# Own attention of layers 0 and 2 in slots of several batches, and the beginnings of the tiled attention stages

## The chip, the cores and the metric

One core of one Trainium2 chip runs the whole kernel. A core has five engines that run their own instruction lists and meet only at semaphores: TensorE (PE in the profile; its weight loads stand apart as PEld), VectorE (DVE), ScalarE (ACT), GpSimd (POOL) and SyncE (SP), which issues the DMAs. TensorE writes eight banks of PSUM (0 to 7), from which VectorE and ScalarE read. The metric is the time of one execution on the device, in microseconds.

## What is computed

A decoder of four layers on `x` of 8 batches, 112 positions and 256 features, all in float32, with a context `ctx` of 8 × 375 × 128. Each layer adds own attention, cross attention and a feed-forward part, each on a layer norm of `x`. The parts that the change touches:

```python
# layer 0, own attention: 16 query heads, 4 key/value heads of 64
v = hn @ Wv.T + bv
q = relu(lstm_q(hn) @ Wq1.T + bq1) @ Wq2.T + bq2
k = relu(lstm_k(hn) @ Wk1.T + bk1) @ Wk2.T + bk2
k, v = repeat(k, 4), repeat(v, 4)
scores = where(causal, q @ k.T / 8, lowest)
y = concat(softmax(scores) @ v) @ Wo.T

# layer 2, own attention: 8 query heads, 4 key/value heads of 128, no bias
q, k, v = hn @ Wq, hn @ Wk, hn @ Wv
q, k = q * cos + rotate_half(q) * sin, k * cos + rotate_half(k) * sin
scores = where(causal, q @ repeat(k, 2).T / sqrt(128), -inf)
y = concat(softmax(scores) @ repeat(v, 2)) @ Wo
```

Of the other stages (own attention of layer 1, cross attention of layers 1 and 3, the two attention blocks of layer 2) the change touches the order of their first batch alone.

## The kernel before

**Stages.** The program is one stage after another. In a stage, a class gives one list of steps (`order()`), each a name with a batch and an index, and every engine walks through the same list and issues its own part of each step: `pe()`, `act()`, `dve()` and `pool()` of `Attention`. So the list sets the order on every engine, and semaphores hold an engine until the other one's part is done. `k.project` (L248) is a sum of matmuls over the feature tiles, `k.tp` (L253) a transpose on TensorE. One matmul in float32 stands as two instructions in the profile, one transpose as one. `k.next_bank` gives out the banks of a ring and waits until the last reader of that bank is done; `k.fill` does so for a fixed bank.

**Own attention of layers 0 and 2** (`L0Attn`, `L2Attn`, both on `Attention`). A batch's heads are taken in groups of four (4 groups in layer 0, 2 in layer 2). For a group: *scores* on TensorE into bank 0 or 1, 448 wide; *weigh*: VectorE adds the triangle to the four heads and writes them to memory (L639), takes the negated maxima (L645), and ScalarE computes four exponentials of 112x112 with their sums (L592); *turn*: four transposes of the weights (L253) into bank 4 or 5 and VectorE's copy (L659); *values*: the turned weights are TensorE's stationary side, the values move, and the result has queries on its partitions (banks 6 and 7). After a batch's last group, *divide* takes the reciprocals of the sums (L676) and scales the result out of the banks (L698, one instruction per bank of 512); *oT* turns it by eight transposes, copied by VectorE (L705); *y* multiplies with the output weights (two matmuls of 8 tiles, 256 moving, L248), and VectorE adds it to `x` (L756). The parts of the next batch (the *prologue*) and the end of the last one (the *epilogue*) are dealt by `Slots` over the gaps between these steps. The next batch's first group of scores stands ahead of the last group's values:

```python
            if b + 1 < B:
                yield from self.scoring(b + 1, 0, None)
            yield "values", b, self.G - 1
            yield "divide", b, 0
```

*Layer 0's prologue:* hid twice (112 positions by 64 on TensorE, relu on VectorE, L1480), queries twice (four tiles of 128 with a contraction of 64, L1456), keys (L1463) and v (L248). The contraction of the scores is 64 deep, while a tile of the queries holds two heads on 128 partitions. So VectorE writes each query tile twice, once with the one head and once with the other zeroed (L1486, scalar `q_mask`), and the score product takes all 128 rows. Keys are L1493. The scale of 1/8 is in the mask.

*Layer 2's prologue:* stats (VectorE, L764 to L769, then GpSimd's power, L790), xn (L774), xT (two transposes, copy L777), three rotations of four heads each (products of 128 x 112 on TensorE; VectorE two half-height products with sine, L1735, and one with cosine, L1737; GpSimd the sum, L1744), and v (512 wide). Scores of batch b wait for all three sums of b.

**Tiled stages** (`Tiled`: cross attention of layers 1 and 3, `L2Block2`; `TiledSelf`: `L1Attn`, `L2Block1`). Their heads of 16 or 32 are taken four at a time by row pieces of 32 for scores (L886, L1134) and column pieces of 32 for values (L912, L1158), with exponentials from L934 and L1174. The list has a *prologue* for batch 0, the first scores, then *second*, which is always of batch 1, then the loop with a *plan* of what goes into each gap. In `prologue`, k with an index is a piece of the keys, v a chunk of the values, vv two chunks at once. `dve_parity` (L1020 to L1028) begins stages with heads of 16: VectorE makes a mask for even and odd heads, then zeroes both value buffers (L1025, 128x1536 elements each in a cross stage, 112x512 in layer 1's attention), ahead of the first statistics. Queries are evacuated twice, once per parity (L1040). L1007 is GpSimd's copy that shares out the reciprocals, L1218 its product of 112x448, and L1182 ScalarE's copy of turned weights.

## Time and profile before

| | |
|---|---|
| median of 3 runs | 2730.49 us (2727.94 to 2737.71) |
| profiled execution | 2720.24 us, span 2718.4 us |
| mean granted clock | 0.828 of full |
| TensorE busy (PE / weight loads) | 2137.2 us (79%) / 1549.3 us |
| VectorE | 1506.7 us (55%) |
| ScalarE | 816.4 us (30%) |
| GpSimd | 336.0 us (12%) |
| chain that ended last | PE 60%, issue 16%, DVE 15%, POOL 3%, ACT 3%, DMA 2% |

The busy shares are means over stages that are bound differently, so they tell little of one stage. The chain (followed back from the last instruction to what released each step) is TensorE for six tenths and VectorE for three twentieths. The granted clock is TensorE's: 1 is full, 2.4 GHz, and 0.5 its lower level, 1.2 GHz; the mean of 0.828 holds stretches at either. Times in the trace count from the start of the span.

### The profile page before, as it was taken

Reading aid. Unit: us, or ns where it says so; the run is one execution under the profiler, and the core shown is the slowest. Engines: PE = TensorE matmul, PEld = TensorE weight load, DVE = VectorE, ACT = ScalarE, POOL = GpSimd, SP = SyncE. Lnnn points to the kernel's source line nnn. Section 1 sums busy time; section 2 is a strip of 40 time slices with the busy share of each in tenths; the row PEclk is TensorE's granted clock in tenths of the full one; section 3 lists DMA queues with packets and bytes.
Section 4 is the critical chain, followed back from the end, with each engine's and each line's share of the span. In section 5 each row is a group of like instructions: output and inputs, shape, how many; then the busy total and the mean of one; then the engine's idle time right before and its main releaser. Section 6 shows DMA issues by size and latency. Waiting matters only on the chain.

```text
span 2718.4 us, 56558 instructions
## 1 busy us (share of the span) xinstructions
PE 2137.2 (79%) x22836; PEld 1549.3 (57%) x22836; DVE 1506.7 (55%) x4047; ACT 816.4 (30%) x2897; POOL 336.0 (12%) x601
## 2 busy tenths in 40 slices
PE   7788888896777789478777387799889999879824
PEld 4777777774446566345666265566554544546612
DVE  5777776653424578643465264277617040358788
ACT  1333333221214556211111044156411111226511
POOL 2111111000000100000111153033100000210011
PEclk9555555987988889689899698899999999769956
DMA  2000001003000000200000200000011000000000
GB/s 116 4 4 4 4 4 67 1 1 141 14 0 1 7 10 10 117 0 1 4 1 1 124 1 1 6 10 8 4 72 59 0 0 0 1 9 13 5 0 14
DMA packets 7744, 57.14 MB, mean 21 GB/s; under 512 B 760, under 2 KB 5216, under 8 KB 5728
## 3 DMA queue, kind: packets, MB, share of 16 engines
q1 hardware_dynamic: 7488, 53.54, 5.1%
q8 instruction: 184, 3.01, 0.5%
q14 instruction: 72, 0.59, 0.1%
HBM read 52.62 MB, written 0.92 MB: 20 GB/s over the span
## 4 chain that ended last, share of the span: by engine, by line
PE 60%; issue 16%; DVE 15%; POOL 3%; ACT 3%; DMA 2%; POOLq 0%; DVEq 0%; SPq 0%; ACTq 0%
PE banks L248 35%; PE banks L1292 11%; PE banks L253 8%; PE banks L886 2%; PE banks L912 2%; DVE memory L1191 1%; ACT memory L934 1%; DVE memory L774 1%; DVE memory L972 1%; DMA memory<-in_l2x_rows 1%; DVE memory L698 1%; DVE memory L2302 1%; DVE memory L1394 1%; DVE memory L764 1%; PE banks L1456 1%
## 5 line engine op out<-in xcount | busy, mean ns | idle before, releaser
L248 PE MATMUL banks<-memory 128*128 128x448 f32 (+10 forms) x5040 | 1288.1, 412 | 123.6 <-DMA memory<-in_ctxT 16.9
L248 PEld LDWEIGHTS banks<-memory 128*128 128x128 f32 (+4 forms) x5040 | 828.8, 199 | 492.6 <-issue 260.1
L253 PE MATMUL banks<-memory 112*125 112x112 f32 (+3 forms) x2128 | 346.3, 296 | 249.9 <-DVE memory L774 124.2
L253 PEld LDWEIGHTS banks<-memory 112*125 112x125 f32 (+3 forms) x2128 | 264.2, 177 | 372.0 <-issue 185.1
L1292 PE MATMUL banks<-memory 128*128 128x8 bf16 (+2 forms) x10752 | 306.2, 174 | 75.8 <-DVE memory L1394 74.4
L1292 PEld LDWEIGHTS banks<-memory 128*128 128x128 bf16 x10752 | 295.3, 104 | 87.4 <-DVE memory L1394 85.3
L934 ACT ACTIVATE memory<-banks,memory 112x375 f32<-112x375 f32 x384 | 215.1, 578 | 17.2 <-DVE memory L972 17.1
L972 DVE TENSOR_REDUCE memory<-banks 112x2 f32<-112x750 f32 x192 | 171.1, 934 | 50.0 <-PE banks L886 48.1
L592 ACT ACTIVATE memory<-memory 112x112 f32<-112x112 f32 x192 | 72.1, 376 | 262.4 <-DVE memory L645 262.4
L790 POOL TENSOR_TENSOR memory<-memory 112x1 f32<-112x1 f32 x88 | 48.3, 549 | 790.0 <-DVE memory L769 788.5
L980 DVE COPY memory<-banks 125x448 f32<-125x448 f32 x192 | 116.7, 619 | 14.5 <-PE banks L253 10.2
L1377 DVE TENSOR_REDUCE memory<-banks 128x64 f32<-128x256 f32 x224 | 95.1, 425 | 27.5 <-PE banks L1292 1.6
L1316 ACT ACTIVATE memory<-memory 128x64 f32<-128x64 f32 x224 | 57.4, 256 | 171.7 <-DVE memory L1377 171.7
L886 PE MATMUL banks<-memory 32*112 32x375 f32 x768 | 89.8, 537 | 16.4 <-ACT memory L934 15.9
L1341 POOL TENSOR_SCALAR memory<-memory 128x16 f32<-128x16 f32 x224 | 59.8, 267 | 344.0 <-DVE memory L1394 344.0
L956 ACT COPY memory<-banks 125x448 f32<-125x448 f32 x96 | 51.1, 532 | 136.5 <-PE banks L253 136.5
L2659 DVE TENSOR_TENSOR memory<-banks,memory 112x256 f32<-112x256 f32 x8 | 3.4, 425 | 159.5 <-PE banks L248 159.5
L1174 ACT ACTIVATE memory<-banks,memory 112x112 f32<-112x112 f32 x256 | 86.2, 390 | 4.8 <-DVE memory L1191 3.4
L934 ACT ACTIVATION_READ_ACCUMULATOR memory<-banks,memory 112x1 f32 x384 | 80.6, 210 | 0.0
L912 PE MATMUL banks<-memory 125*32 125x112 f32 x2304 | 76.8, 267 | 1.4 <-DVE memory L980 1.4
L606 ACT COPY memory<-banks 128x375 f32<-128x375 f32 (+1 forms) x56 | 27.2, 485 | 150.7 <-PE banks L248 150.7
L2637 ACT ACTIVATE memory<-banks,memory 128x448 f32<-128x448 f32 x32 | 20.3, 633 | 173.5 <-PE banks L248 173.5
(202 smaller groups left out, 2126.4 us busy)
## 6 DMA issues: line engine op xcount, KB each, us to landing
memory<-in_l2x SPq DMA_DIRECT2D x1, 7680.0 KB, 21.2
memory<-in_l2f SPq DMA_DIRECT2D x1, 7168.0 KB, 19.6
memory<-in_l1f SPq DMA_DIRECT2D x1, 4617.0 KB, 17.0
memory<-in_ctxT SPq DMA_DIRECT2D x24, 187.5 KB
memory<-in_l0a SPq DMA_DIRECT2D x1, 4224.0 KB, 15.8
memory<-in_l2f SPq DMA_DIRECT2D x1, 4096.0 KB, 12.9
memory<-in_l3f SPq DMA_DIRECT2D x1, 3073.0 KB, 22.1
memory<-in_l2a SPq DMA_DIRECT2D x1, 3072.0 KB, 23.9
```

The source lines that it names most:

```text
L248: ins = self.nc.tensor.matmul(out, weights[i], acts[i], start=i == 0, stop=i == n - 1)
L253: return self.nc.tensor.transpose(out, in_, self.ident[0:n, 0:n])
L592: A.activation(P_sb[:, h, :], src[:, h, :], ACT.Exp, bias=u["nmax"][:, n + h:n + h + 1], scale=1.0, accum_out=u["total"][:, n + h:n + h + ...
L886: ins = PE.matmul(k.bank(bank, S, CK), q, kT, start=True, stop=True)
L912: ins = PE.matmul(k.banks[32 * r:32 * r + 32, 6, t * S:(t + 1) * S], v, PT_sb[0:CR, c, r * S:(r + 1) * S], start=c == 0 and m == 0, stop=c ...
L934: self.nc.scalar.activation(self.P_both[gi % 2][:, r, :], self.k.bank(r, S, CK), ACT.Exp, bias=u["nmax"][:, 4 * i + r:4 * i + r + 1], scal ...
L972: V.tensor_reduce(u["nmax"][:, 4 * i + 2 * h:4 * i + 2 * h + 2], k.banks[0:S, 2 * h:2 * h + 2, 0:CK], AX, ALU.max, negate=True).then_inc(* ...
L980: V.tensor_copy(self.PT_both[gi % 2][0:CR, c, :], k.bank(k.at["turn", gi, c], CR, 4 * S)).then_inc(*s.pt_v.up())
L1174: A.activation(self.P_all[:, i, g, :], k.bank(i, S, 4 * S)[:, g * S:(g + 1) * S], ACT.Exp, bias=u["nmax"][:, 4 * i + g:4 * i + g + 1], sca ...
L1292: ins = self.nc.tensor.matmul(self.slots[l][:, part:3, g * B:(g + 1) * B], whh[:, part, l, j, g * P:(g + 1) * P], self.upper[l][:, 0:3 - p ...
L1341: G.tensor_scalar(self.hs[:, l, :, :, t], self.h[:, l, 0].rearrange("p (k b) -> p k b", k=KD), 0.5, None, ALU.mult).then_inc(*s.h_kept.up())
L1377: V.tensor_reduce(self.sums[:, l], self.slots[l].rearrange("p s c -> p c s"), AX, ALU.add).then_inc(*s.gates_in.up())
```

## The change

**A new class `Causal`** carries both attentions. Its unit is eight heads: half a batch in layer 0, a whole one in layer 2. The steps of several batches stand in one slot (a tuple of step, index, and lag in batches), and the slot is repeated.

```diff
+class Causal(Attention):
...
+        self.ring = (2, 3, 4, 5)
...
+            if step == "sc":
...
+                for h in range(2):
+                    k.fill(h, s.exp_done(8 * n + 4 * h + 4))
+                    PE.matmul(k.bank(h, S, 4 * S), k.ident[0:S, 0:S],
+                              k.causal[0:S, :].unsqueeze(1).broadcast_to([S, 4, S]), start=True, stop=False,
+                              skip_group_check=True)
+                for j in range(4):
+                    for h in range(2):
+                        q, kT = self.score(b, i, h, j)
+                        ins = PE.matmul(k.bank(h, S, 4 * S)[:, j * S:(j + 1) * S], q, kT, start=False, stop=True,
+                                        skip_group_check=True)
+                ins.then_inc(*s.sc_full.up())
+            elif step == "turn":
+                for h in range(2):
+                    PE.wait_ge(*s.diag_ready(2 * n + h + 1))
+                    bank = k.next_bank(("turn", n, h), s.pt_ready(2 * n + h + 1))
+                    for j in range(4):
+                        ins = PE.matmul(k.bank(bank, S, 4 * S)[:, j * S:(j + 1) * S], self.P[n % 2][:, h, j, :],
+                                        self.diag[n % 2][:, h, j, :], start=True, stop=True)
+                    ins.then_inc(*s.pt_full.up())
...
+            if step == "exp":
+                for h in range(2):
+                    A.wait_ge(*s.nmax_ready(2 * n + h + 1))
+                    if n >= 2:
+                        A.wait_ge(*s.pt_full(2 * (n - 2) + h + 1))
+                        A.wait_ge(*s.inv_ready(n - 1))
+                    for j in range(4):
+                        at = 4 * h + j
+                        A.activation(self.P[n % 2][:, h, j, :], k.bank(h, S, 4 * S)[:, j * S:(j + 1) * S], ACT.Exp,
+                                     bias=self.nmax[n % 2][:, at:at + 1], scale=1.0,
+                                     accum_out=self.total[n % 2][:, at:at + 1]).then_inc(*s.exp_done.up())
...
+            if step == "max":
+                V.wait_ge(*s.sc_full(n + 1))
+                for h in range(2):
+                    V.tensor_reduce(self.nmax[n % 2][:, 4 * h:4 * h + 4],
+                                    k.bank(h, S, 4 * S).rearrange("p (h n) -> p h n", h=4), AX, ALU.max,
+                                    negate=True).then_inc(*s.nmax_ready.up())
+            elif step == "inv":
+                V.wait_ge(*s.exp_done(8 * (n + 1)))
+                if n >= 2:
+                    V.wait_ge(*s.diag_ready(2 * (n - 1)))
+                V.reciprocal(self.inv[n % 2], self.total[n % 2]).then_inc(*s.inv_ready.up())
...
+            if step == "inv":
+                G.wait_ge(*s.inv_ready(n + 1))
+                for h in range(2):
+                    if n >= 2:
+                        G.wait_ge(*s.pt_full(2 * (n - 2) + h + 1))
+                    G.tensor_tensor(self.diag[n % 2][:, h], k.ident[0:S, 0:S].unsqueeze(1).broadcast_to([S, 4, S]),
+                                    self.inv[n % 2][:, 4 * h:4 * h + 4].unsqueeze(2).broadcast_to([S, 4, S]),
+                                    ALU.mult).then_inc(*s.diag_ready.up())
```

So the triangle is written to the bank by a product with the identity, 448 wide, and the score products add to it; exponentials read the bank; the weights are multiplied by a diagonal matrix of the reciprocals, which turns and divides them at once; and the diagonals are made by GpSimd, a product of 112x448 with both operands broadcast. P, diag, nmax, total and inv have two buffers each, PT has one. The ring is banks 2 to 5.

**Layer 0.** The slot of a batch has an even and an odd unit. Scores and values use half the array: the two heads of a tile are row pieces of 64 in the scores, and column pieces of 64 in the values, so that the result has features on its partitions and needs no turning. VectorE writes the queries once.

```diff
+class L0Attn(Causal):
...
+    EVEN = (("y", 0, 3), ("turn", 0, 2), ("sc", 0, 1), ("max", 0, 1), ("exp", 0, 1), ("hid", 0, 0), ("hid", 1, 0),
+            ("values", 0, 2), ("queries", 0, 0), ("inv", 0, 1))
+    ODD = (("turn", 1, 2), ("sc", 1, 1), ("max", 1, 1), ("exp", 1, 1), ("keys", 0, 0), ("values", 1, 2),
+           ("queries", 1, 0), ("v", 0, 0), ("inv", 1, 1))
...
         self.w, self.bias, self.hs = lstm.w, lstm.bias, lstm.hs
...
-        self.o, self.oT = take(4 * D, parts=S), take(8, S)
-        self.q_mask, self.bq2m = take(2), take(2, 8)
-        self.take_common(take, [dict(qm=take(8, 2, S), kT=take(4, S), v=take(1, D, parts=S)) for _ in range(2)])
...
+        self.r1, self.bq2s = take(2, S, parts=64), take(8)
+        self.q, self.kT = [take(8, S) for _ in range(2)], [take(4, S) for _ in range(2)]
+        self.v, self.oT = [take(D, parts=S) for _ in range(3)], [take(8, S) for _ in range(2)]
...
+    def score(self, b, i, h, j):
+        rows = slice(64 * h, 64 * h + 64)
+        return self.q[b % 2][rows, 4 * i + j, :], self.kT[b % 2][rows, 2 * i + j // 2, :]
...
+        elif step == "values":
+            n = 2 * b + i
+            PE.wait_ge(*s.v_ready(b + 1))
+            PE.wait_ge(*s.pt_ready(2 * (n + 1)))
+            bank = 6 + n % 2
+            k.fill(bank, s.oT_ready(n + 1))
+            for j in range(4):
+                for h in range(2):
+                    at = 64 * (2 * i + j // 2)
+                    ins = PE.matmul(k.banks[64 * h:64 * h + 64, bank, j * S:(j + 1) * S], self.v[b % 3][:, at:at + 64],
+                                    self.PT[:, h, j, :], start=True, stop=True)
+            ins.then_inc(*s.val_full.up())
...
+        if step == "values":
+            n = 2 * b + i
+            A.wait_ge(*s.val_full(n + 1))
+            if b >= 2:
+                A.wait_ge(*s.y_full(b - 1))
+            A.copy(self.oT[b % 2][:, 4 * i:4 * i + 4, :].rearrange("p t s -> p (t s)"),
+                   k.bank(6 + n % 2, P, 4 * S)).then_inc(*s.oT_ready.up())
...
-            for m in range(2):
-                ins = V.scalar_tensor_tensor(
-                    out=u["qm"][:, 4 * i:4 * i + 4, m, :], in0=ps, scalar=self.q_mask[:, m:m + 1],
-                    in1=self.bq2m[:, m, 4 * i:4 * i + 4].unsqueeze(2).broadcast_to([P, 4, S]),
-                    op0=ALU.mult, op1=ALU.add)
-            ins.then_inc(*s.q_ready.up())
+            V.scalar_tensor_tensor(out=self.q[b % 2][:, 4 * i:4 * i + 4, :], in0=ps, scalar=0.125,
+                                   in1=self.bq2s[:, 4 * i:4 * i + 4].unsqueeze(2).broadcast_to([P, 4, S]),
+                                   op0=ALU.mult, op1=ALU.add).then_inc(*s.q_ready.up())
...
+        elif step == "turn":
+            n = 2 * b + i
+            for h in range(2):
+                V.wait_ge(*s.pt_full(2 * n + h + 1))
+                if n:
+                    V.wait_ge(*s.val_full(n))
+                self.copy_turned(V.tensor_copy, n, h).then_inc(*s.pt_ready.up())
```

**Layer 2.** The values' product has the values stationary, so here too its result needs no turning. ScalarE takes the copies of the turned weights, of the result, of v and of xT. VectorE keeps statistics, xn, rotations, maxima, reciprocals and the sum with `x`.

```diff
-class L2Attn(Attention):
...
+class L2Attn(Causal):
...
-    epilogue = (("oT", 0), ("oT", 1), ("y", 0))
...
+    SLOT = (("y", 0, 4), ("turn", 0, 3), ("sc", 0, 2), ("max", 0, 2), ("stats", 0, 0), ("exp", 0, 2), ("rot", 0, 1),
+            ("values", 0, 3), ("rot", 1, 1), ("xn", 0, 0), ("rot", 2, 1), ("v", 0, 1), ("xT", 0, 0), ("inv", 0, 2))
...
+    def score(self, b, i, h, j):
+        n = 4 * h + j
+        return self.q[b % 2][:, n, :], self.kT[b % 2][:, n // 2, :]
...
+        elif step == "values":
+            PE.wait_ge(*s.v_ready(b + 1))
+            for h in range(2):
+                PE.wait_ge(*s.pt_ready(2 * b + h + 1))
+                k.fill(6 + h, s.oT_ready(2 * b + h + 1))
+                for j in range(4):
+                    at = P * ((4 * h + j) // 2)
+                    ins = PE.matmul(k.bank(6 + h, P, 4 * S)[:, j * S:(j + 1) * S], self.v[b % 3][:, at:at + P],
+                                    self.PT[:, h, j, :], start=True, stop=True)
+                ins.then_inc(*s.val_full.up())
...
+        if step == "turn":
+            for h in range(2):
+                A.wait_ge(*s.pt_full(2 * b + h + 1))
...
+                self.copy_turned(A.copy, b, h).then_inc(*s.pt_ready.up())
+        elif step == "values":
+            for h in range(2):
+                A.wait_ge(*s.val_full(2 * b + h + 1))
+                if b:
...
+                A.copy(self.oT[b % 2][:, 4 * h:4 * h + 4, :].rearrange("p t s -> p (t s)"),
+                       k.bank(6 + h, P, 4 * S)).then_inc(*s.oT_ready.up())
+        elif step == "v":
+            A.wait_ge(*s.v_full(b + 1))
...
+            A.copy(self.v[b % 3], k.bank(k.at["v", b], S, self.KV * P)).then_inc(*s.v_ready.up())
+        elif step == "xT":
+            A.wait_ge(*s.xT_full(b + 1))
...
+            A.copy(self.xT[b % 2].rearrange("p j s -> p (j s)"),
+                   k.bank(k.at["xT", b], P, KD * S)).then_inc(*s.xT_ready.up())
...
+        if step == "stats":
+            self.dve_stats(k.x[:, b, :])
+        elif step == "xn":
+            if b:
+                V.wait_ge(*s.xT_full(b))
+            self.dve_norm(k.x[:, b, :], self.xn).then_inc(*s.xn_ready.up())
...
+            if b >= 2:
+                V.wait_ge(*s.sc_full(b - 1))
```

**Beginnings.** `second` now names its batch, and parts of batch 0 stand there, behind the first scores; in `L2Block2` the order ahead of them changes too. The two memsets go from VectorE to GpSimd, and the first evacuation of the values waits for them (`zeroed(2)`, in `dve_value` and `dve_values`).

```diff
-        for kind, i in self.second:
-            yield kind, 1, i
+        for kind, i, b in self.second:
+            yield kind, b, i
```

```diff
-        for u in self.bufs:
-            ins = V.memset(u["v"], 0.0)
...
+    def pool_begin(self):
+        if self.par:
+            for u in self.bufs:
+                self.nc.gpsimd.memset(u["v"], 0.0).then_inc(*self.s.zeroed.up())
```

The lists of cross attention, `L1Attn`, `L2Block1` and `L2Block2`, in this order:

```diff
-    prologue = (("stats", 0), ("xn", 0), ("k", 0), ("xT", 0), ("q", 0), ("k", 1), ("vv", 0), ("v", 2))
-    second = (("stats", 0),)
+    prologue = (("stats", 0), ("xn", 0), ("k", 0), ("xT", 0), ("q", 0))
+    second = (("k", 1, 0), ("vv", 0, 0), ("v", 2, 0), ("stats", 0, 1))
...
-    prologue = (("stats", 0), ("xn", 0), ("xT", 0), ("k", 0), ("q", 0), ("v", 0))
-    second = (("stats", 0), ("xn", 0), ("xT", 0))
+    prologue = (("stats", 0), ("xn", 0), ("xT", 0), ("k", 0), ("q", 0))
+    second = (("v", 0, 0), ("stats", 0, 1), ("xn", 0, 1), ("xT", 0, 1))
...
-    prologue = (("ln", 0), ("xm", 0), ("stats", 0), ("xn", 0), ("xT", 0), ("k", 0), ("q", 0), ("v", 0))
-    second = (("ln", 0), ("xm", 0), ("stats", 0), ("xn", 0), ("xT", 0))
+    prologue = (("ln", 0), ("xm", 0), ("stats", 0), ("xn", 0), ("xT", 0), ("k", 0), ("q", 0))
+    second = (("v", 0, 0), ("ln", 0, 1), ("xm", 0, 1), ("stats", 0, 1), ("xn", 0, 1), ("xT", 0, 1))
...
-    prologue = (("cstat", 0), ("ln", 0), ("cn", 0), ("xm", 0), ("cT", 0), ("stats", 0), ("k", 0), ("xn", 0), ("k", 1),
-                ("xT", 0), ("k", 2), ("q", 0), ("v", 0), ("v", 1))
-    second = (("ln", 0), ("xm", 0), ("stats", 0))
+    prologue = (("ln", 0), ("xm", 0), ("cstat", 0), ("stats", 0), ("cn", 0), ("xn", 0), ("xT", 0), ("q", 0), ("cT", 0),
+                ("k", 0), ("k", 1))
+    second = (("k", 2, 0), ("v", 0, 0), ("v", 1, 0), ("ln", 0, 1), ("xm", 0, 1), ("stats", 0, 1))
```

## Rows read from the trace of the kernel before

**Rows 1.** Windows of four stretches; the first line names the columns.

```profile
core 0: us, PE busy (x) PEld busy (x) DVE busy (x) ACT busy (x) POOL busy (x), PEclk, DMA share, GB/s
453.80:642.90 189.10, 166.69 (x1120) 142.76 (x1120) 113.35 (x212) 50.93 (x256) 0.00 (x0) 0.88 0.06 24
1311.10:1506.50 195.40, 151.78 (x942) 125.96 (x942) 112.38 (x218) 26.79 (x129) 30.99 (x31) 0.91 0.00 1
...
504.40:511.30 6.90, 6.21 (x21) 4.58 (x19) 2.50 (x5) 1.59 (x8) 0.00 (x0) 0.51 0.01 2
1112.00:1173.00 61.00, 17.36 (x63) 12.73 (x62) 36.57 (x165) 3.45 (x10) 2.03 (x2) 0.50 0.31 129
```

**Rows 2.** Chain of waits, one batch of layer 0's attention (start, us, what).

```profile
500.60 0.64 DVE memory L639
...
506.46 7.56 PE banks L248 x28
```

**Rows 3.** Timeline of TensorE (PE), two batches of the same stage.

```profile
477.43 2.92 PE L248 MATMUL banks<-memory 112*112 112x64 f32 x28
...
485.06 5.20 PE L248 MATMUL banks<-memory 128*112 128x256 f32 x28 [1.27 <-DVE memory L705]
...
498.82 2.92 PE L248 MATMUL banks<-memory 112*112 112x64 f32 x28
```

**Rows 4.** Timeline, layer 2's attention; in brackets idle before, releaser.

```profile
1405.10 1.26 DVE L1735 TENSOR_TENSOR memory<-banks,memory 64x448 f32<-64x448 f32 x2
...
1409.00 1.13 POOL L1744 TENSOR_TENSOR memory<-memory 128x448 f32<-128x448 f32 x1 [0.80 <-DVE memory L1737]
```

**Rows 5.** Groups by line, layer 0's stage, then layer 2's; last the idle before.

```profile
L592 ACT ACTIVATE memory<-memory 112x112 f32<-112x112 f32 x128 | 48.0, 376 | 124.7 <-DVE memory L645 124.7
...
L698 DVE TENSOR_TENSOR memory<-banks,memory 112x512 f32<-112x512 f32 x16 | 10.3, 686 | 1.2 <-DVE memory L676 1.0
...
L592 ACT ACTIVATE memory<-memory 112x112 f32<-112x112 f32 x64 | 24.0, 377 | 137.8 <-DVE memory L645 137.7
```

**Rows 6.** TensorE's pieces that the prices are taken from, in five stretches.

```profile
857.16 1.06 PE L248 MATMUL banks<-memory 128*128 128x112 f32 x8
...
1393.62 3.72 PE L248 MATMUL banks<-memory 128*112 128x256 f32 x16 [0.47 <-DVE memory L705]
...
2263.77 6.07 PE banks L248 x16
...
513.86 0.55 PE L253 MATMUL banks<-memory 112*112 112x112 f32 x4
...
515.79 1.14 PE L1456 MATMUL banks<-memory 64*128 64x112 f32 x8
...
516.86 1.04 PE L248 MATMUL banks<-memory 128*112 128x112 f32 x8
...
860.29 1.05 PE L1134 MATMUL banks<-memory 32*112 32x112 f32 x32
...
863.01 0.97 PE L1158 MATMUL banks<-memory 112*32 112x112 f32 x32
```

**Rows 7.** Single lines (xcount: duration ns min/median/max, first and last start).

```profile
L1182 ACT COPY memory<-banks x48: 531/532/635, 845.7 to 1676.0; 112x448 f32<-112x448 f32 x48
...
L1218 POOL TENSOR_TENSOR memory<-memory x32: 979/983/987, 1548.1 to 1672.2; 112x448 f32<-112x448 f32 x32
...
L1007 POOL COPY memory<-memory x40: 397/398/643, 850.7 to 2577.4; 112x256 f32<-112x256 f32 x24, 112x512 f32<-112x512 f32 x16
...
L1025 DVE MEMSET memory<- x6: 485/1338/1338, 827.9 to 2411.2; 128x1536 f32 x4, 112x512 f32 x2
```

**Rows 8.** Timeline, layer 1's cross attention: power, q's evacuation, first scores.

```profile
943.46 0.55 POOL L790 TENSOR_TENSOR memory<-memory 112x1 f32<-112x1 f32 x1 [7.17 <-DVE memory L769]
...
947.73 0.81 DVE L1040 SCALAR_TENSOR_TENSOR memory<-banks,memory 128x224 f32<-128x224 f32 x2 [2.15 <-PE banks L248]
...
951.46 0.94 PE L886 MATMUL banks<-memory 32*112 32x375 f32 x8
```

209 lines of the change are left out of this document (144 added, 65 removed).

## The prediction

> **How the profile was read.** The chip runs one long program of stages, and the diff touches seven of them, so the span is cut by stage first. The windows [rows 1] give layer 0's own attention 189.1 us (453.8 to 642.9) and layer 2's own 195.4 us (1311.1 to 1506.5). TensorE is busy 166.7 and 151.8 us of them, at a mean granted clock of 0.88 and 0.91 of full. Neither stage is at TensorE's limit, and the next question is who holds it up.
>
> The chain of waits answers it. In one batch of layer 0 [rows 2] the chain leaves TensorE for 5.9 us (500.57 to 506.46): mask add, maximum, reciprocal, the two scalings L698, four transposes, a copy, and only then TensorE again. All of it but the transposes is VectorE, one after the other, and TensorE did only some 1.6 us of work meanwhile. The x28 that follows took 7.56 us where the same 28 instructions one batch before took 5.20 [rows 3]: the granted clock fell to its lower level, 1.2 GHz, right after that light stretch (0.51 in 504.4 to 511.3 [rows 1]). In layer 2 the same chain runs through statistics, xn, xT and three rotations, each of two L1735 (1.26), one L1737 of half that and GpSimd's add (1.13) [rows 4], before scores may start.
>
> The groups [rows 5] show the slack of the others: ScalarE idles 124.7 and 137.7 us, in two stages of 190, until a maximum is out.
>
> **Prices, at the full clock** [rows 6]. I take an instruction's price as (time from first start to last end, less one duration of 0.26 or so) over the count less one. A product of float32 is two instructions, a transpose one. Weights 112 wide: 28 in 2.92 us [rows 3], so 0.099 us. Weights 128 wide, 112 moving: 8 in 1.06, so 0.111. 256 moving: 16 in 3.72, so 0.216. 448 moving: 16 in 6.07, so 0.38. Transposes: 4 in 0.55, so 0.097. Four row pieces of 32 at a time: 32 in 1.05, so 0.102 for four; four column pieces: 32 in 0.97, so 0.092 for four. Two at a time cost the same per turn by these rows, so 0.051 and 0.046 each. Going from 64-row to full weights or back: 8 instructions from 515.79 to 516.86 are 1.07 us where 8 × 0.111 is 0.89. So 0.18 to 0.19 us for a switch.
>
> The Trainium skill (TensorEngine Tiling (Array Packing), Key Properties) says that a change of tiling mode drains TensorE, which speaks against this change; it gives no figure. By that rule the trace agrees, 0.19 us at each switch; without it the sum for layer 0 would be 1.7 us a batch lower.
>
> **Layer 0, one batch.** *Before:* 8 instructions of hid at about 0.10 (0.8), 24 of queries and keys (2.7), 32 of scores (3.2), 16 transposes of weights (1.6), 32 of values (3.2), v (0.9), 8 transposes oT (0.8), y (3.5), 6 switches (1.1): 17.6 us. The undisturbed batch is 21.4 us (477.43 to 498.82 [rows 3]), one with the lower clock 23.7.
> *After:* hid 0.8, queries and keys 2.7, v 0.9, y 3.5 stay. Added: four triangles through the identity, 448 wide, 8 × 0.38 = 3.0. Scores in two row pieces 32 × 0.051 = 1.6 (less 1.6). Turning by a diagonal is a product, not a transpose: 32 × 0.099 = 3.2 (plus 1.6). Values in two column pieces 32 × 0.046 = 1.5 (less 1.7), oT gone (less 0.8). 9 switches 1.7. Sum 18.8: TensorE gets more work, not less.
> What goes is VectorE's share of the chain. VectorE loses four mask adds of 0.64 [rows 2], two scalings of 0.69 [rows 5], two copies of oT and half of L1486's four passes, which are of the mask add's size: 6.5 us a batch of the 113.35 / 8 = 14 [rows 1]. ScalarE gets two copies (0.53 [rows 7]) on top of 16 exponentials at 0.38 [rows 5], some 7 us in all. GpSimd gets four diagonals of 112x448 at 0.98 (L1218 [rows 7]), 3.9 us. All lie beside TensorE, and with turn a whole batch behind inv the diagonals have some 10 us to spare. If that cover went, a late diagonal would cost its full time.
> Stalls left: scores use one pair of banks, so from the end of one unit's scores to the next's second bank there are 0.27 + maxima + eight exponentials, about 4.1 us; other TensorE work between is 4.5 or more, no stall. Queries wait for hid's relu, queued behind the two maxima on VectorE: 0.4. y waits for ScalarE's copy of the values, queued behind eight exponentials: scores' end + 4.75, TensorE is there at 3.5: 1.2. With 0.4 for the other waits: 20.8 a batch.
> Whole stage: the first projections as now to 462.4; the first two units cannot cover the 4.1 us loop, 8.7 us to 471.1; a batch without y 14.6; five batches of 20.8; then 18.1 to the last scores and 20.2 from there (exponentials, y 3.5, turn, copy 0.9, values, turn, copy, values, copy, y): 628. Light stretches at both ends put the clock down, for which I add 5: 633 against 642.9. **Gain 9 to 10**, I take 9.
>
> **Layer 2, one batch.** *Before:* rotations' products 48 × 0.111 = 5.3, y 3.5, v 1.8, scores 1.6, values 1.8, transposes 0.8 + 0.8 + 0.2: 15.7 of 23.9 us. *After:* masks 4 × 0.38 = 1.5, turn 16 × 0.099 = 1.6 (plus 0.8), oT gone: 17.3. VectorE keeps three rotations of 1.9, maxima 1.2, statistics, xn and y, about 9; ScalarE gets turn, xT, v and value copies, about 6.4; GpSimd 3 × 1.13, two diagonals of 1.0 and 0.55, about 6. The rotations belong to the batch one slot later, xT to two slots, so the chain from statistics to the add is spread over slots. The closest race is GpSimd's: TensorE does values, two rotations, v and xT (7.3 us after rot 0's end) and y, and wants the diagonals at 10.8 and 11.6; VectorE ends the last rotation at 8.1 (0.3 + 1.9, then with TensorE's pace 6.2 + 1.9), GpSimd's add 9.4, the diagonals 10.4 and 11.4. It just fits. With 0.6 for waits, 17.9 a slot.
> Whole stage: first projections 10.5 us (at the lower level, as now), then a wait for the add of about 1.5 and 10.9; then 13.8 without y; five slots of 17.9; 8.1 to the last scores; from there 17.7 (exponentials, y, turn, copies, values, copy, y). That is 1463; with 6 for the lower clock at both ends 1469.5, against 1506.5. **Gain 37.**
>
> **Beginnings of five tiled stages** [rows 8]. In cross attention of layer 1 the first scores start at 951.46, q's last evacuation ends at 948.54: moving k 1 and v behind the scores gives 2.8; the moved 4 us lie in TensorE's idle while the exponentials run, and if that cover were gone they would cost what they gave. The same reading of the three others with something moved gives 1.8 (layer 3), 0.9 (first block of layer 2) and, where k 2 and v stood before the scores and the order is new, about 2 (second block). The memsets leave VectorE, 2.7 us in each cross stage (1.34 each [rows 7]). A memset on GpSimd isn't in the trace; its copies of 256 and 512 are 0.40 and 0.64 [rows 7], 0.96 ns an element, so about 1.6 for 1536, two 3.3. Its power, queued behind them, starts at about 941.9 instead of 943.46: 1.5 each, which I take as its nearest row. The ends: 2.2 (at VectorE's price, when TensorE's k 0 holds xT), and -2 (twice a copy's price per element). First attention of layer 1: 1.0, its memsets being a third. Sum 11.5, **I take 11.** The loops behind are the same, so a start saved is an end saved.
>
> **Sum.** 9 + 37 + 11 = 57. The profiled execution took 2720.24 us (span 2718.4), 10.25 below the median 2730.49; so 2663 beside the profile, and 2674 as a median.
>
> **Rivals.**
> *A. GpSimd becomes the bound in layer 2.* If a diagonal with both operands broadcast costs 2.4 us and not 1.0, the second ends at 14.2 and turn stalls 2.6 us a slot: 21 lost, 2695. For: the race above is within 0.4 us. Against: L1218 [rows 7] has the same size and one broadcast operand, 0.98. 0.10.
> *B. The clock keeps falling.* Mean clocks of 0.88 and 0.91 over 189 and 195 us are 45 and 35 us at the lower level now. If the new waits keep it there, both stages lose 12 to 15 us each of the gain: 2700. For: it fell after light stretches of 2 to 4 us, and new ones exist at both ends. Against: in the steady state TensorE is over 85% busy. 0.12. The Trainium skill (TensorE: Matmul & The Clock Gate, A second HAM failure mode) tells of a kernel whose cycling through PSUM banks made short idles and clock changes, which is what a ring of four banks could do; the trace bears it out only after long stretches, not short ones.
> *C. Slower: the steady state runs at the lower level.* TensorE's sums then double, 37.6 and 34.5 a batch; the stages become 120 and 85 us longer in place of 46 shorter: about 2920. It decides as soon as the lower level lasts 114 us longer than now, since each us there costs half. For: 61 us at 0.50 exist (1112 to 1173 [rows 1]). Against: TensorE is busy 17 of those 61. 0.03.
> *D. Less concurrency.* If two row or column pieces run one after the other, layer 0 gets 3.1 us a batch dearer, 25 in all: 2699. For: rows exist only for four pieces. Against: those ran fully at once. 0.05.
> *E. The ends lose nothing to the clock and the starts give 15:* 2655. 0.08.
> The change doing something other than it says (a stage started by the same waits as now) would leave about 2720: 0.02.
>
> **Numbers.** The forecast has 0.60, its own range 2660 to 2690. With A, B, D and E, each with its own spread of some 10 us, 8 in 10 lie in 2655 to 2704. About 0.5% (13.7 us) is what a measurement of this kernel can tell from no change. Faster by more than that: all but C and the last, 0.95; within 0.5% 0.02; slower 0.03.
>
> **What the profile after would show.** Windows of the two stages near 180 and 158 us, clocks above 0.95 in their middles; turn of two instructions and about 0.1 each; mask products 448 wide at 0.38; a y in layer 0 that waits about 1.2 us for ScalarE's copy; L2's turn waiting at most 0.2 for GpSimd; first scores in the cross stages some 4 us after today's distance less. Wrong: TensorE waits on GpSimd for over a microsecond a slot (A), clock under 0.9 mid-stage (B, C), scores of layer 0 at 0.1 an instruction (D).

## The result and the profile after

The changed kernel takes **2646.24 us** (median of 4 runs, 2632.98 to 2649.78) where the kernel before takes 2729.6 (4 runs, 2727.94 to 2737.71): a ratio of 0.969, 95% interval 0.9653 to 0.9727. The forecast was 2674, so the sign was right and the size, 56 us for a measured 83, fell short; the time lies under the range. The profiled execution took 2649.78 us (span 2648.1), 70.5 us under the profiled one of before. Two later runs of the kernel before, of 2766 and 3060 us at mean clocks of 0.79 and 0.67, are left out of all comparisons.

First the windows of the changed kernel, for the two rebuilt stages (they answer to [rows 1]) and for the stage between them that the diff doesn't touch, layer 0's cross attention. Columns as in [rows 1].

```profile
453.80:617.30 163.50, 156.59 (x1248) 122.49 (x1248) 66.10 (x137) 51.78 (x272) 29.30 (x32) 0.96 0.07 28
1284.50:1442.00 157.50, 146.28 (x976) 123.46 (x976) 66.50 (x144) 46.05 (x177) 46.61 (x48) 0.95 0.00 1
...
617.30:722.90 105.60, 69.68 (x258) 47.04 (x258) 38.70 (x124) 16.54 (x40) 4.44 (x8) 0.82 0.26 99
```

The same stretch of cross attention in the kernel before:

```profile
642.80:743.20 100.40, 65.63 (x258) 44.33 (x258) 38.74 (x124) 16.51 (x40) 4.42 (x8) 0.86 0.27 105
```

Layer 0's stage fell from 189 to 163.5 us and layer 2's from 198.8 (from its first instruction of any engine on) to 157.5. VectorE's busy time in them went from 113 to 66 us each, TensorE's down by 10 and 6 only, and the granted clock rose from 0.88 and 0.91 to 0.96 and 0.95. Cross attention of layer 0 has the same instructions on every engine and took 5.2 us more, at a clock of 0.82.

Part of layer 0's gain came with the clock. In the kernel before, TensorE spent 43.8 us of this stage at the lower level, now 13.2. A batch there took 21.4 us without any of it and 23.6 to 23.8 us with 6.8 us of it, 0.34 us for each; at that price the 30.6 us are worth some 10 of the 25.4 (an estimate). The fall goes with the new form: in its eleven profiles the stage holds 7 to 19 us at the lower level, in the three of the old form 37 to 53.

Where the 70.3 us of the two spans went, stage by stage, each from its first instruction to the next stage's:

| stage | before | after | gain | forecast |
|---|---|---|---|---|
| layer 0, own attention | 188.9 | 163.5 | 25.4 | 9 |
| layer 2, own attention | 198.8 | 157.5 | 41.3 | 37 |
| cross attention, layers 1 and 3 | 185.0 + 172.7 | 179.7 + 166.7 | 11.3 | together 11 |
| blocks 1 and 2 of layer 2 | 238.5 + 282.6 | 235.2 + 281.4 | 4.5 | |
| layer 1, own attention | 111.2 | 112.5 | -1.3 | |
| all others, not touched | | | -10.9 | 0 |

The steady state tells the most. One slot of layer 0 on TensorE, in the changed kernel's timeline:

```profile
530.26 1.74 PE L1460 MATMUL banks<-memory 112*112 112x112 f32 x16
531.83 1.68 PE L1446 MATMUL banks<-memory 112*112 112x448 f32 x4
533.44 1.04 PE L1452 MATMUL banks<-memory 64*112 64x112 f32 x16
534.41 0.89 PE L251 MATMUL banks<-memory 128*64 128x112 f32 x7
535.04 0.31 PE L1602 MATMUL banks<-memory 112*64 112x112 f32 x1
535.13 0.26 PE L251 MATMUL banks<-memory 128*64 128x112 f32 x1
535.19 0.97 PE L1602 MATMUL banks<-memory 112*64 112x112 f32 x15
536.09 1.14 PE L1579 MATMUL banks<-memory 64*128 64x112 f32 x8
...
540.43 1.04 PE L1452 MATMUL banks<-memory 64*112 64x112 f32 x16
541.31 1.05 PE L1586 MATMUL banks<-memory 64*128 64x112 f32 x8
542.29 0.99 PE L1602 MATMUL banks<-memory 112*64 112x112 f32 x16
543.21 1.14 PE L1579 MATMUL banks<-memory 64*128 64x112 f32 x8
544.28 4.88 PE L251 MATMUL banks<-memory 128*112 128x256 f32 x20
549.00 0.56 PE L1460 MATMUL banks<-memory 112*112 112x112 f32 x4
```

It goes from turn (L1460) over the triangle (L1446, two instructions a bank), scores (L1452), hid, values (L1602), queries (L1579), the odd unit with keys (L1586), v and y (together the x20) to the next turn, 549.00 - 530.26 = 18.74 us, with no bracket of idle time anywhere. The window of such a slot has TensorE busy in all but 0.06 us of it:

```profile
530.40:549.14 18.74, 18.68 (x159) 14.69 (x158) 8.18 (x17) 6.45 (x34) 3.66 (x4) 1.00 0.00 1
1366.60:1383.80 17.20, 17.20 (x124) 14.68 (x123) 8.28 (x18) 5.56 (x22) 5.83 (x6) 1.00 0.01 1
```

The second line is a slot of layer 2, of 17.19 us. The forecast's sums for TensorE alone were 18.8 and 17.3; its slots, stalls included, 20.8 and 17.9. The steady stretch of layer 0 (464.7 to 597.0) ran at a mean clock of 1.00.

### The profile page after: what moved, and what is told of

Read it like the earlier page. It is cut to its first block, busy times and chain, and to the rows that moved or that the text cites. A ratio compares the mean times of both kernels' runs of the same rounds, so it can differ in the third digit from the quotient of the medians.

```text
span 2648.1 us, 56908 instructions
## 1 busy us (share of the span) xinstructions
PE 2127.4 (80%) x22996; PEld 1529.0 (58%) x22996; DVE 1408.7 (53%) x3887; ACT 837.0 (32%) x2961; POOL 387.8 (15%) x655
## 4 chain that ended last, share of the span: by engine, by line
PE 46%; issue 13%; DVE 11%; POOL 3%; ACT 2%; DMA 2%; POOLq 0%; DVEq 0%; ACTq 0%; SPq 0%
PE banks L251 31%; PE banks L256 6%; PE banks L890 2%; PE banks L916 2%; DVE memory L1200 1%; DVE memory L777 1%; DMA memory<-in_l2x_rows 1%; DVE memory L976 1%; DMA memory<-in_ctxT 1%; DVE memory L2523 1%; ACT memory L938 1%; PE banks L1460 1%; DVE memory L767 1%; DVE memory L984 1%; POOL memory L3106 1%
## 5 line engine op out<-in xcount | busy, mean ns | idle before, releaser
L251 PE MATMUL banks<-memory 128*112 128x256 f32 (+9 forms) x4272 | 1188.5, 434 | 113.7 <-DMA memory<-in_ctxT 17.9
L251 PEld LDWEIGHTS banks<-memory 128*128 128x128 f32 (+5 forms) x4272 | 734.7, 200 | 470.6 <-issue 264.7
L256 PE MATMUL banks<-memory 112*125 112x112 f32 (+2 forms) x1808 | 292.5, 294 | 200.0 <-DVE memory L777 116.6
L256 PEld LDWEIGHTS banks<-memory 112*125 112x125 f32 (+2 forms) x1808 | 223.7, 179 | 316.9 <-issue 184.2
L1483 ACT ACTIVATE memory<-banks,memory 112x112 f32<-112x112 f32 x192 | 65.0, 365 | 123.1 <-DVE memory L1497 123.1
L1183 ACT ACTIVATE memory<-banks,memory 112x112 f32<-112x112 f32 x256 | 86.4, 391 | 9.0 <-DVE memory L1200 7.5
L1330 ACT ACTIVATE memory<-memory 128x16 f32<-128x16 f32 x224 | 48.3, 216 | 79.6 <-DVE memory L1395 79.6
## 6 DMA issues: line engine op xcount, KB each, us to landing
memory<-in_l2f SPq DMA_DIRECT2D x1, 4096.0 KB, 13.2
```

The costliest lines, as they stand in the source:

```text
L251: ins = self.nc.tensor.matmul(out, weights[i], acts[i], start=i == 0, stop=i == n - 1)
L256: return self.nc.tensor.transpose(out, in_, self.ident[0:n, 0:n])
L1183: A.activation(self.P_all[:, i, g, :], k.bank(i, S, 4 * S)[:, g * S:(g + 1) * S], ACT.Exp, bias=u["nmax"][:, 4 * i + g:4 * i + g + 1], sca ...
L1483: A.activation(self.P[n % 2][:, h, j, :], k.bank(h, S, 4 * S)[:, j * S:(j + 1) * S], ACT.Exp, bias=self.nmax[n % 2][:, at:at + 1], scale=1 ...
```

## The experiments

**Three parts by themselves.** Each run keeps one part and takes the other two back to the form of before.

```diff
 # only layer 0: L2Attn, the lists and the memsets as before
-class L2Attn(Causal):
+class L2Attn(Attention):
...
 # only layer 2: L0Attn, the lists and the memsets as before
-class L0Attn(Causal):
+class L0Attn(Attention):
...
 # only the beginnings: both classes as before
```

> Only layer 0's attention in the new form; layer 2's attention, the lists of the tiled stages and the memsets as before. Theory (TensorE never waits in the new slot, so the part is worth the whole 25.5 us that its stage got shorter by): slot 18.74 us, stage 163.5 us against 189, time about 25 us under the kernel before, less what the stages behind lose by the clock (the cross stage behind took 5.2 us more in the profile of the change): ratio 0.990 to 0.993. Rival (the part is worth what was forecast, 9 us, and the rest came from elsewhere, as a luckier clock): ratio 0.997.

> Only layer 2's attention in the new form. Theory: slot 17.19 us, stage 157.5 against 198.8 us, time about 41 us under the kernel before, ratio 0.985. Rival (as forecast, 37 us): 0.9865; the two are told apart by the slot in the trace, 17.2 or 17.9 us, rather than by the ratio.

> Only the lists of the tiled stages and the memsets on GpSimd. Theory: the five stages get shorter by some 11 us together (cross of layer 1 by 5.3, of layer 3 by 2, the first block of layer 2 by 3.3, the second by 1.2, layer 1's own attention by nothing), ratio 0.996. Rival (a start saved is given back inside the stage, as layer 1's own attention shows, 1.3 us longer after the change): ratio 0.999 or more.

Measured, as ratios to the kernel before: layer 0 alone 0.9894 (0.9865 to 0.9924, 2695.28 us), layer 2 alone 0.9838 (0.9809 to 0.9866, 2680.4), beginnings alone 0.9953 (0.9931 to 0.9974, 2710.08). Their product is 0.969, the ratio of the whole: within these intervals the parts are additive. Layer 0's ratio lies just under the 0.990 to 0.993 that were expected, and 0.997 and 0.999, the rivals of the first and the third run, are outside the intervals. Layer 0's slots are 18.73 us and its stage 163.2 in a program where nothing else differs:

```profile
454.20:617.40 163.20, 156.42 (x1248) 122.39 (x1248) 66.07 (x137) 51.65 (x272) 29.26 (x32) 0.96 0.07 28
```

So the part is worth 25 us in its stage and the rival, 9 us and luck, falls. Layer 2's slots are 17.19, as expected. The beginnings gave 5.3 and 5.7 us in the two cross stages, where 5.3 and 2 were expected.

**How much room is there behind ScalarE?** The forecast let y wait 1.2 us a batch for ScalarE's copy of the values. This run makes that copy twice.

```diff
+            A.copy(self.oT[b % 2][:, 4 * i:4 * i + 4, :].rearrange("p t s -> p (t s)"),
+                   k.bank(6 + n % 2, P, 4 * S)).then_inc(*s.astep.up())
+            A.wait_ge(*s.astep.now())
             A.copy(self.oT[b % 2][:, 4 * i:4 * i + 4, :].rearrange("p t s -> p (t s)"),
                    k.bank(6 + n % 2, P, 4 * S)).then_inc(*s.oT_ready.up())
```

> The changed kernel, with ScalarE's copy of layer 0's turned-free values (0.57 us) made twice, 16 more copies. The trace of the change shows y start 0.22 us late, right when this copy ends, so there is no slack left in the odd unit. Theory (my stall terms were right in place and too long by the exponentials' price, 0.38 for a pitch of 0.33): each batch gets longer by the whole second copy, its wait included, 0.6 to 0.7 us, slot 19.35 to 19.45, stage 5 us longer. Rival (y's start is TensorE's own pace and the copy has room): slot 18.74.

The slot became 19.31 us, 0.57 more (0.6 to 0.7 were expected), and the wait now shows in its timeline, ahead of y:

```profile
545.92 1.12 PE L251 MATMUL banks<-memory 128*112 128x256 f32 x4
547.66 2.63 PE L251 MATMUL banks<-memory 128*112 128x256 f32 x11 [0.62 <-ACT memory L1616]
```

The edge is there, then, right where the forecast put it, and the schedule stands just on it. It was the length of the wait that was wrong. The exponentials and the copy in the changed kernel, odd unit:

```profile
542.18 0.35 ACT L1483 ACTIVATE memory<-banks,memory 112x112 f32<-112x112 f32 x1 [3.77 <-DVE memory L1497]
...
542.53 0.34 ACT L1483 ACTIVATE memory<-banks,memory 112x112 f32<-112x112 f32 x1
...
544.50 0.39 ACT L1483 ACTIVATE memory<-banks,memory 112x112 f32<-112x112 f32 x1
...
544.83 0.57 ACT L1613 COPY memory<-banks 128x448 f32<-128x448 f32 x1
```

Scores end at 541.47 (540.43 + 1.04), the first exponential starts at 542.18, eight of them lie 0.33 us apart (7 in 542.18 to 544.50), and the copy ends at 545.40: 3.93 us behind the scores, where I had 4.75. TensorE's last product of v starts at 545.02, so it is through at 545.23, 3.76 behind the scores where I had 3.5, and y, at 545.46, waits 0.22.

**Are GpSimd's diagonals covered?** Each is made twice.

```diff
-                    G.tensor_tensor(self.diag[n % 2][:, h], ...).then_inc(*s.diag_ready.up())
+                    for up in (s.gstep, s.diag_ready):
+                        G.tensor_tensor(self.diag[n % 2][:, h], ...).then_inc(*up.up())
+                        if up is s.gstep:
+                            G.wait_ge(*s.gstep.now())
```

> The changed kernel, with each of GpSimd's diagonals (0.92 us) made twice, in both layers. Theory: layer 0's are needed six us or more after they are ready and cost nothing (slot 18.74); layer 2's second one ends at 1383.78 where its four products start at about 1384.4, 0.6 us of slack, so two more of 0.92 make its turn some 1.2 us late and the slot 17.19 becomes 18.3 to 18.5, its stage 8 us longer. Rival (the forecast's race, which left 0.2 and less): slot 18.9 or more. Second rival: no cover in layer 0 either, slot over 20.

Layer 0's slot stayed at 18.73 us, layer 2's went from 17.19 to 18.74, 1.55 more and somewhat over what was expected:

```profile
1369.98 1.04 PE L1460 MATMUL banks<-memory 112*112 112x112 f32 x8 [0.18 <-POOL memory L1527]
1371.88 1.04 PE L1460 MATMUL banks<-memory 112*112 112x112 f32 x8 [0.86 <-POOL memory L1527]
```

Two more products are about 1.86 us of GpSimd and cost 1.55, so layer 2 had 0.3 us of slack, not the 0.6 that I read off the changed trace. Rival A's "within 0.4 us" was a fair reading. In the change the products took 0.92 us each and the race was won:

```profile
1380.86 1.13 POOL L1965 TENSOR_TENSOR memory<-memory 128x448 f32<-128x448 f32 x1 [1.01 <-DVE memory L1954]
1381.95 1.83 POOL L1526 TENSOR_TENSOR memory<-memory 112x448 f32<-112x448 f32 x2
```

**Do the pieces of the array work side by side?** The order of the products alone is changed, in scores and values:

```diff
-                for j in range(4):
-                    for h in range(2):
+                for h in range(2):
+                    for j in range(4):
```

> The changed kernel, with the two row pieces of layer 0's scores, and the two column pieces of its values, one after the other (all four products of the one, then of the other) and not in turns. Theory (what halves the price to 0.051 and 0.047 us is that neighbours in the list work on different pieces of the array): 32 scores and 32 values of a batch go from 3.2 to 6.3 us, slot 18.74 to 21.8. Rival (the price is that of the smaller tile, whatever the order): slot 18.74.

The slot became 20.13 us: 1.39 longer, so the order matters, but by under half of what the theory said. The rows:

```profile
538.11 1.52 PE L1452 MATMUL banks<-memory 64*112 64x112 f32 x16
...
540.38 1.37 PE L1602 MATMUL banks<-memory 112*64 112x112 f32 x16
```

By the count of instructions a score product costs (1.52 - 0.26) / 15 = 0.084 us in this order and one of the values 0.074, in turns 0.052 and 0.049 ((1.04 - 0.26) / 15 and (0.99 - 0.26) / 15). But 0.084 is a mean of two things. The first four and the last three of the same sixteen score instructions:

```profile
538.11 0.64 PE L1452 MATMUL banks<-memory 64*112 64x112 f32 x4
...
539.17 0.46 PE L1452 MATMUL banks<-memory 64*112 64x112 f32 x3
```

The last ones, of the second piece alone, start 0.098 us apart, by the row (0.46 - 0.26) / 2 = 0.10, and so do the second to fifth of the first piece: the price of the whole array. In between, the second piece's first instruction starts 0.006 us behind the first piece's fifth, and from there the two run side by side. So this order doesn't put the pieces wholly in series, it takes away half of the overlap, and the slot lost 1.39 of the 3.1 us that the theory and rival D had for all of it. (The rows of both steps add to 1.7 us a slot; 0.15 of the difference is y's wait, 0.22 before and 0.07 here.) Rival D is excluded by the change's own rows: in turns a pair of score instructions starts every 0.098 us, what one alone takes. D's price of 3.1 us stands as an estimate, from 0.098 for 0.049.

**TensorE's list as the only bound.** If no wait is left, each instruction taken from TensorE must shorten the slot by its price. Two edits of that kind: the mask's product in bf16 (its operands are zeros, ones and one large number, of which only the size matters), and a turn by plain transposes, for which GpSimd multiplies the weights in place by the reciprocals.

```diff
-                    PE.matmul(k.bank(h, S, 4 * S), k.ident[0:S, 0:S],
-                              k.causal[0:S, :].unsqueeze(1).broadcast_to([S, 4, S]), start=True, stop=False,
+                    PE.matmul(k.bank(h, S, 4 * S), self.ident16,
+                              self.causal16.unsqueeze(1).broadcast_to([S, 4, S]), start=True, stop=False,
...
+        V.tensor_copy(self.ident16, k.ident[0:S, 0:S]).then_inc(*s.zeroed.up())
+        V.tensor_copy(self.causal16, k.causal[0:S, :]).then_inc(*s.zeroed.up())
```

```diff
-                        ins = PE.matmul(k.bank(bank, S, 4 * S)[:, j * S:(j + 1) * S], self.P[n % 2][:, h, j, :],
-                                        self.diag[n % 2][:, h, j, :], start=True, stop=True)
+                        ins = k.tp(k.bank(bank, S, 4 * S)[:, j * S:(j + 1) * S], self.P[n % 2][:, h, j, :])
...
-                    G.tensor_tensor(self.diag[n % 2][:, h], k.ident[0:S, 0:S].unsqueeze(1).broadcast_to([S, 4, S]),
+                    G.tensor_tensor(self.P[n % 2][:, h], self.P[n % 2][:, h],
```

> The changed kernel with the identity and the triangle of the mask product in bf16 (each triangle one instruction in place of two at 0.38 us). Theory (TensorE is the bound in both slots, with no wait but 0.22 us for y): one bf16 product of 448 columns is at most half of a float32 pair's half, some 0.19 to 0.38 us, so a slot of layer 0 loses 1.5 to 2.3 us (18.74 to 16.4 to 17.2) and one of layer 2 0.8 to 1.1 us (17.19 to 16.1 to 16.4), 18 to 27 us in all, ratio 0.990 to 0.993 of the changed kernel. Rival (the loop over the pair of score banks, 4.1 us by the forecast, or y's wait for ScalarE is the bound as soon as TensorE does less): the slot of layer 0 stays over 18 us and the gain is under 8 us.

> The changed kernel, where GpSimd multiplies the weights themselves by the reciprocals (448 elements, one operand broadcast, in place) and not the identity, and TensorE turns them by plain transposes, 8 instructions a unit in place of 16. Theory (TensorE's list of instructions is the slot): 1.6 us less in layer 0 (18.74 to 17.15) and 0.8 less in layer 2 (17.19 to 16.4), 19 us in all, ratio 0.993 of the changed kernel, whatever the product costs GpSimd up to 1.0 us. Rival (GpSimd's product of two read operands takes over 1.2 us, and layer 2's second one comes late, as in the run with the product twice): slot of layer 2 17.2 or more.

With the bf16 triangle the slots were 16.47 and 16.06 us: 2.27 and 1.13 less, which is 8 × 0.38 - 4 × 0.19 = 2.28 and half of it. The time was 2624.11 us (0.9624 of the kernel before, 0.9593 to 0.9655). The rival, that a bank loop or y's wait binds as soon as TensorE does less, is out: y's wait stayed at 0.22. With the transposes they were 17.08 and 16.39 (1.66 and 0.80 less), the time 2626.04 (0.9637, 0.9611 to 0.9663). Its turn, 0.93 us for a unit where it was 1.74, from the run with both:

```profile
545.68 0.93 PE L256 MATMUL banks<-memory 112*112 112x112 f32 x8
546.45 0.54 PE L1450 MATMUL banks<-memory 112*112 112x448 bf16 x2
546.92 1.04 PE L1456 MATMUL banks<-memory 64*112 64x112 f32 x16
```

GpSimd's product of two read operands took 0.94 us, like the diagonal's.

**The memsets.** Two runs move them: back to VectorE, and on GpSimd behind the first xn.

```diff
 # back on VectorE, in dve_parity, as before
+        for u in self.bufs:
+            ins = V.memset(u["v"], 0.0)
...
-                self.nc.gpsimd.memset(u["v"], 0.0).then_inc(*self.s.zeroed.up())
```

```diff
 # behind xn, in Attention.pool
+            if step == "xn" and zero:
+                zero = False
+                G.wait_ge(*s.xn_ready(1))
+                for v in self.bufs:
+                    G.memset(v["v"], 0.0).then_inc(*s.zeroed.up())
```

> The changed kernel with the two memsets of the stages with heads of 16 back on VectorE, all else as in the change. In the trace of the change VectorE's two small products L1026 and L1030 took 1.10 and 1.31 us beside GpSimd's memset of 2.72, where they took 0.17 and 0.23 before. Theory (GpSimd's memset holds VectorE up, so the move gives only the difference): the small products are back at 0.17 and 0.23, first statistics of cross attention at 3.96 us from the stage's start where they are at 2.78 now, the two cross stages 1.2 us longer each. Rival (the move was worth the whole 2.7 us of the memsets): 2.7 us longer each.

> The changed kernel, with GpSimd's memsets behind the first xn and not at the stage's start, all else as in the change. Theory (VectorE's products in memory wait while GpSimd's memset runs, its reads of banks don't): L1026 and L1030 back at 0.17 and 0.23 us, first scores of layer 1's cross attention at 7.0 to 7.6 us from the stage's start in place of 8.80. Rival (VectorE's evacuations into memory are held up too): 8.8 or more, with the evacuations of xT and q longer than 0.39 and 0.81.

Beginning of layer 1's cross attention in the changed kernel:

```profile
921.15 2.72 POOL L1037 MEMSET memory<- 128x1536 f32 x2 [2.20 <-DVEq L263]
...
921.45 1.10 DVE L1026 TENSOR_SCALAR memory<-memory 128x2 f32<-128x2 f32 x1
922.59 1.31 DVE L1030 TENSOR_SCALAR memory<-memory 128x2 f32<-128x2 f32 x2
...
929.98 1.61 PE L890 MATMUL banks<-memory 32*112 32x375 f32 x8 [0.90 <-DVE memory L1047]
```

VectorE's tiny products end at 922.55 and 923.90, just when GpSimd's first and second memset end (922.5 and 923.87). With the memsets on VectorE L1026 took 0.17 us, and the first scores came 10.06 us behind the stage's start, with them on GpSimd 8.80. So the move is worth 1.3 us here, where the theory had 1.2 and the rival 2.7. It is worth 0.8 in layer 1's own attention and 2.0 in layer 3, where only one of the two products exists. The stage as a whole, though, didn't get longer by 1.2 us as expected: it was 178.6 us with the memsets on VectorE and 179.7 in the change, at 22 us of the lower clock in the one and 30 in the other. Layer 3's got longer, 169.3 for 166.7. Behind xn the memsets disturb nothing:

```profile
918.17 0.17 DVE L1031 TENSOR_SCALAR memory<-memory 128x2 f32<-128x2 f32 x1
...
920.33 0.41 DVE L777 TENSOR_SCALAR memory<-memory 112x256 f32<-112x256 f32 x1 [0.73 <-POOL memory L798]
920.80 2.70 POOL L794 MEMSET memory<- 128x1536 f32 x2 [0.51 <-DVE memory L777]
920.93 1.59 PE L251 MATMUL banks<-memory 128*128 128x375 f32 x2 [4.09 <-DMA memory<-in_ctxT]
...
922.32 0.58 PE L256 MATMUL banks<-memory 112*128 112x112 f32 x2
922.93 0.39 DVE L780 COPY memory<-banks 128x224 f32<-128x224 f32 x1 [2.19 <-PE banks L256]
```

The evacuation L780 kept its 0.39 us beside the memset, yet first scores came at 8.44 and not at 7.0 to 7.6: xn is ready at 920.74, but k 0 has just started on TensorE when ctx landed, and xT waits behind its 1.6 us. The next bound was the one that the forecast had named in half a sentence, and that this expectation left out.

**Better versions.** All three edits (bf16 triangle, transposes, memsets behind xn), and then the same with another order of layer 0's slot:

```diff
-    EVEN = (("y", 0, 3), ("turn", 0, 2), ("sc", 0, 1), ..., ("hid", 1, 0), ("values", 0, 2), ("queries", 0, 0), ("inv", 0, 1))
-    ODD = (..., ("keys", 0, 0), ("values", 1, 2), ("queries", 1, 0), ("v", 0, 0), ("inv", 1, 1))
+    EVEN = (("turn", 0, 2), ("y", 0, 3), ("sc", 0, 1), ..., ("hid", 1, 0), ("values", 0, 2), ("v", 0, 0), ("inv", 0, 1))
+    ODD = (..., ("keys", 0, 0), ("queries", 0, 0), ("queries", 1, 0), ("values", 1, 2), ("inv", 1, 1))
```

> The changed kernel with the bf16 triangle, the turn by transposes, and the memsets on GpSimd behind xn instead of at the stage's start. Theory: the savings of TensorE's list add up, layer 0's slot 18.74 - 2.27 - 1.6 = 14.9, layer 2's 17.19 - 1.13 - 0.8 = 15.3; first scores of cross attention 1.2 to 1.9 us sooner; together 42 us under the changed kernel, about 2604, ratio to the kernel before 0.955. Rival (the loop over the pair of score banks, 3.7 us from the last score of a unit to the last exponential, is now longer than what TensorE has between, 3.6): slot of layer 0 15.3 or more, gain 38.

> The version with all three, and layer 0's slot in another order: queries next to keys, v behind the even unit's values, y behind the first turn, so that TensorE changes between full, row and column pieces 6 times a slot and not 8. Theory (0.19 us a switch, and y's wait of 0.22 covered): slot 0.4 to 0.6 us under the version before it, stage 3 to 5 us less. Rival (queries and keys in one row wait for VectorE's evacuations, and the reordered list stalls): slot as before it or longer.

All three: 2590.4 us, 0.9519 of the kernel before (0.9491 to 0.9546), slots 14.82 and 15.25, so the savings add up here too and the loop over the score banks doesn't bind. The time lies 14 us under the 2604 that was expected, and most of that isn't the edits': in the two profiles, three stretches with the same steps (cross attention of layer 0, the second block of layer 2, and what follows it up to layer 3's cross attention) are 4.7, 5.4 and 7.7 us shorter, with 64 us at the lower level in the last where the change had 89. With fewer switches: **2587.65 us**, 0.9499 (0.9477 to 0.9521), slot 14.24, stage of layer 0 126.2 us where the version before it had 134.3. Two switches of 0.18 and y's wait of 0.22, gone here, make 0.58, what the slot lost. Of the stage's 8.1 us, 3.5 are the steady slots, 1.8 its end and 2.8 its beginning; there the lower level lasted 10.3 us in the one and 4.0 in the other, so most of these 2.8 can't be put down to the order. The two ratios' intervals overlap, so in the whole time the last step is not shown; in the slot it is.

## Why the prediction fell short

It missed by 27.8 us in the median, in two nearly equal halves.

**From profile to median, 14.5 us.** The sum gave 2663 us beside the profile, against 2649.78 measured. To this the forecast added the 11 us by which the profiled execution of before lay under its median. That of the changed kernel lay 3.5 over its own. The kernel before took 2711.46 to 2737.23 us in 26 later runs, so one profile can stand anywhere within some 13 us of the median, and the distance of one kernel's profile is no property of the next. The range took in none of this.

**In the sum itself, 13.3 us:** layer 0 +16.4, layer 2 +4.3, beginnings +3.5, the other stages -10.9.

*Layer 0.* The failed step is the line "stalls left: ... 20.8 a batch". TensorE's own work, 18.8 in the sum, was 18.5 (18.74 less the wait of 0.22; eight switches, not nine, are most of that); the stalls, 2.0, were 0.22. Of its terms, queries waiting for the relu (0.4) don't exist, since the sixteen instructions of the values stand between them; y's wait for the copy (1.2) is 0.22, because the exponentials were priced by their duration, 0.38, when they lie 0.33 apart, the way from the scores to the first of them was taken too long as well, and TensorE gets to y later than forecast, at 3.76 and not 3.5 behind the scores; the lump of 0.4 for "the other waits" is nothing. Over five full slots that is 10.3 us. Most of the rest is the 5 us added for the lower clock at the two ends: at the beginning it was in the measured stretch anyway, and at the end it lasted 3.4 us, which costs at most half of that. Another 0.9 went when 9.9 was taken as 9. The terms of the beginning (471.1, measured 471.22) and of the end (20.2 from the last scores, measured 20.9) held.

*Layer 2.* Same step: 17.3 as a sum, 17.19 measured, and the 0.6 for waits was nothing; 3.5 us over five slots; the last 0.8 I have not traced. That GpSimd's race "just fits" was right, by 0.3 us.

*Beginnings.* First scores came sooner by 4.1 us in layer 1's cross attention (2.8 + 1.5 forecast) and 3.8 in layer 3's, 1.0 in the first block (0.9), 4.0 in the second (2), 0.5 in layer 1's own attention (1.0). "A start saved is an end saved" is the step that doesn't hold to the microsecond: the stages got shorter by 5.3, 6.0, 3.3, 1.2 and -1.3, by where in them the clock fell.

*The clock elsewhere.* Rival B looked for the lower level in the rebuilt stages, where it went away (mean 0.96 and 0.95). It turned up in stages with the same instructions as before. Layer 0's cross attention in seven profiles, its length beside the us at the lower level (twice the length times one minus the mean clock, from the clock's own record):

| kernel | us | at the lower level |
|---|---|---|
| pieces in series | 98.6 | 20.5 |
| bf16 triangle | 98.8 | 20.5 |
| before | 100.4 | 27.3 |
| memsets on VectorE | 104.1 | 34.1 |
| layer 0 alone | 105.6 | 37.5 |
| after | 105.6 | 37.5 |
| fewer switches | 106.1 | 37.5 |

Each us at the lower level costs 0.4: 7 us for 17. Which of these lengths a kernel gets changed with edits in other stages, and I have no rule for it. Why the clock falls where it does stays open; that the 10.9 us lost in untouched stages are the clock's is shown for this stage's 5.2 only. For the others it is argued from one pair of profiles: own attention of layer 3 took 87.2 us for 83.1, with 72 at the lower level for 58, and layer 0's feed-forward part 1.6 us more, with 24 for 20.

Rivals A, C and D are settled: A's price was 0.92 and not 2.4, C's lower level never stood in a steady slot, and for D the pieces run side by side. The nearest to the outcome was E, 2655 at 0.08, and its two conditions came nearly true (3.4 us at the lower level at the end of layer 0, beginnings 14.5). That it came nearest is luck in part: E kept the stalls of 20.8 and 17.9 a slot, and their absence, 13.8 us over ten slots, is in none of the rivals. The forecast should have been the rows' sum with no stall added that no row showed.

Two sums of the prediction come out otherwise: the terms of layer 0's batch before make 17.8 us, not 17.6, and E's 2674 less 11 for the ends and 4 for the starts is 2659. Neither moves the forecast.

## What to carry to other kernels

When a steady state is worked out instruction by instruction, believe the sum of the engine that has the most to do, and price every wait by walking both sides to the same instant from pitches, not durations; lumps for "other waits" and "the clock" cost this forecast some 9 us, its prices of TensorE's instructions some 2. Then ask at what extra time each wait would start to bind, and test that by doubling the covered piece: y had no room at all, GpSimd's second product 0.3 us. Once one engine is busy all the time, the next gains are its cheapest instructions (a mask in bf16, a transpose for a product), and they came out to 0.06 us of the price.
